# A four-layer network over eight batches: another order of its stages, the long kernel's products over four groups of TensorE, and the copy of the scores as a stage of its own

## What is computed

```
x = x + attention(norm(x), context)        8 heads over 64 keys, softmax
x = x + experts16(norm(x))                 sigmoid gates, best 4 of 16 experts, ReLU
x = x + text_layer(norm(x), context)       see below
x = x + experts8(x)                        each of 8 experts takes the best N/8 of all N = 4096 rows
```

```
K[d, l] = 2 Re( sum_n dC[d, n] exp(dtA[d, n] * l) )      256 channels, 64 states, l < 512
y       = irfft(rfft(x) * rfft(K)) + x * D_skip
```

## Time and profile before

| what | value |
|---|---|
| median of 3 runs | 1406.09 us (1405.59 to 1408.57) |
| the profiled execution | 1405.65 us |
| its span, first to last instruction | 1403.8 us |
| mean granted TensorE clock | 0.927 |
| PE busy | 1206.8 us, 86%, 5149 instructions |
| DVE busy | 920.2 us, 66%, 3415 instructions |
| ACT busy | 474.2 us, 34% |
| POOL busy | 341.8 us, 24% |
| DMA, mean | 52 GB/s |

### The profile page before, as it was taken

The page is one execution under the profiler, slowest core; times in us unless marked ns, Lnnn a source line. Parts: engine busy times, 40 slices in busy tenths (PEclk is TensorE's granted clock), DMA queues, the critical chain, the costliest instruction groups (busy, mean ns, idle before and its releaser), DMA issues. The chain is left out here.

```text
span 1403.8 us, 17324 instructions
## 1 busy us (share of the span) xinstructions
PE 1206.8 (86%) x5149; PEld 718.5 (51%) x5149; DVE 920.2 (66%) x3415; ACT 474.2 (34%) x824; POOL 341.8 (24%) x603
## 2 busy tenths in 40 slices
PE   4776967998999899899989979999687439999997
PEld 3543544555456355454546635455264326667664
DVE  6767898778778767768877877787964481211111
ACT  3535431163143326215223441531413423323221
POOL 4323220033023112203212221320203212322332
PEclk9787978999999999899999999999888759999999
DMA  8102002100300300120030040021000135533321
GB/s 281 38 15 61 19 1 69 25 1 16 92 19 1 107 18 1 49 59 19 16 92 19 1 107 15 1 62 38 1 0 0 63 107 165 144 98 91 95 39 19
DMA packets 45351, 72.51 MB, mean 52 GB/s; under 512 B 8549, under 2 KB 27208, under 8 KB 45130
## 3 DMA queue, kind: packets, MB, share of 16 engines
q1 hardware_dynamic: 39114, 62.88, 15.2%
q0 software_dynamic: 6144, 8.52, 3.4%
HBM read 58.27 MB, written 13.07 MB: 51 GB/s over the span
## 5 line engine op out<-in xcount | busy, mean ns | idle before, releaser
L843 POOL TENSOR_SCALAR ve<-mv 128x2 f32<-128x2 f32 x74 | 16.9, 228 | 509.9 <-DVE mv L1111 509.7
L1691 PE MATMUL ps<-x,keys 128*128 128x512 f32 x256 | 124.9, 613 | 4.7 <-DVE hT L1205 4.7
L1862 PE MATMUL ps<-hT,values 128*128 128x512 f32 x256 | 119.1, 594 | 0.0
L2318 PE MATMUL experts_ps<-experts_yT,experts_fc 128*128 128x512 f32 x256 | 111.9, 595 | 1.2 <-ACT experts_yT L2243 1.2
L2330 PE MATMUL experts_ps<-experts_fc,experts_hT 128*128 128x256 f32 x512 | 112.0, 379 | 0.8 <-ACT experts_hT L2255 0.8
L1691 PE MATMUL ps<-zT_second,w 128*128 128x512 f32 x224 | 104.7, 607 | 6.0 <-ACT big L1632 3.9
L2330 PEld LDWEIGHTS experts_ps<-experts_fc,experts_hT 128*128 128x128 f32 x512 | 96.6, 190 | 14.6 <-ACT experts_hT L2255 1.6
L2227 DVE SCALAR_TENSOR_TENSOR experts_o<-experts_ps,experts_wh,experts_b2w 128x256 f32<-128x256 f32 x32 | 15.5, 484 | 128.7 <-PE experts_ps L2330 128.7
L1691 PE MATMUL ps<-w,big 128*128 128x256 f32 x448 | 99.0, 379 | 0.8 <-ACT big L1632 0.8
L2255 ACT ACTIVATE experts_hT<-experts_ps,experts_b 128x512 f32<-128x512 f32 x64 | 44.0, 687 | 155.3 <-PE experts_ps L2318 155.3
L1691 PEld LDWEIGHTS ps<-w,big 128*128 128x128 f32 x448 | 84.1, 190 | 12.5 <-ACT big L1632 1.6
(11 more groups left out here) (445 smaller groups left out, 2388.9 us busy)
## 6 DMA issues: line engine op xcount, KB each, us to landing
gT<-expert_gates SPq DMA_DIRECT2D x32, 512.0 KB, 7.5
experts_fc<-in_fc1T SPq DMA_DIRECT2D x8, 1024.0 KB, 5.1
experts_fc<-in_fc2T SPq DMA_DIRECT2D x8, 1024.0 KB, 8.7
xT<-in_xT SPq DMA_DIRECT2D x8, 512.0 KB, 3.6
x<-in_x SPq DMA_DIRECT2D x8, 512.0 KB, 3.6
expert_table<-tb SPq DMA_DIRECT2D x7, 528.0 KB, 9.7
out_x<-x SPq DMA_DIRECT2D x7, 512.0 KB, 9.1
w<-in_W SPq DMA_DIRECT2D x2, 1024.0 KB, 9.1
```

Source lines behind the costliest of these rows:

```text
L843: nc.gpsimd.tensor_scalar(o, i, c, None, ALU.add).then_inc(*tick(*event))
L1691: last = nc.tensor.matmul(o, l, r_, start=start, stop=stop)
L1862: last = nc.tensor.matmul(bank("O2", k), S["values"][:, c, k * P:(k + 1) * P], hT[:, c % RING, :], start=(c == 0), stop=(c == HC - 1))
L2318: last = nc.tensor.matmul(g_bank(m), fc1[e % 3][:, k, m * P:(m + 1) * P], yT[e % 2][:, k, :], start=(k == 0), stop=(k == DC - 1))
```

## The change

It does three things.

1. The written list has another order. It has 972 entries in place of 948; the new ones are `scores_out` of each batch and `scales` 0 and 1 of each batch. No other stage is added or dropped.
2. `powers` on PE: the 32 products of a pass go to the four groups of 32 output partitions in turn, eight to each. The host puts the channels in an order that makes the result lie as before.
3. The copy of the turned scores leaves `table`. PE's turn and ACT's copy are now the stage `scores_out`; `table` keeps ACT's eight activations. POOL's nine instructions for the scales leave `scores` and become `scales`.

The code:

```diff
+QUARTERS = 4
...
             def scores(b, h):
+                w = room(b)
+                rstd_of(b, LN_EXPERTS, h, w)
+
+            def scales(b, h):
                 ts = pair(h)
                 w = room(b)
                 tr, tmr, tnm, tv, ts2, tnm2 = w.scale
-                rstd_of(b, LN_EXPERTS, h, w)
...
                     nc.scalar.activation(x3[:, t, :], x3[:, t, :], ACT.Identity, bias=w.tnm[:, t, :], scale=w.tr[:, t, :]).then_inc(*tick("x4", t))
+
+            def scores_out(b):
+                w = room(b)
                 a.wait_ge(*w.uses.at(b, "filled", "ST"))
...
             def powers(_, p):
-                lanes = slice((p // 2) * LI, (p // 2 + 1) * LI)
+                each = PC // QUARTERS
                 pe.wait_ge(*at(0, "k_pow", p))
-                for d in range(PC):
-                    last = nc.tensor.matmul(pk[lanes, p % 2, d * LJ:(d + 1) * LJ], Us[p % 2][:, d, :], WAs[p % 2][:, d, :], start=True, stop=True)
+                for r_ in range(each):
+                    place = (p * each + r_) % PC * LJ
+                    for q in range(QUARTERS):
+                        d = q * each + r_
+                        last = nc.tensor.matmul(pk[q * LI:(q + 1) * LI, p // QUARTERS, place:place + LJ], Us[p % 2][:, d, :], WAs[p % 2][:, d, :],
+                                                start=True, stop=True)
                 last.then_inc(*tick("k_taps", p))
...
-            def table(b):
+            def scores_out(b):
                 w = room(b)
                 pe.wait_ge(*at(b, "sc1"))
...
+    for name in ("log_dt", "A_reT", "A_imT", "C_reT", "C_imT"):
+        a = arrays[name]
+        arrays[name] = a.reshape(-1, QUARTERS, PASSES, PC // QUARTERS).transpose(0, 2, 1, 3).reshape(a.shape)
```

More of the change, by code:

```diff
@@ L127 @@
[L127 to L148, removed]
@@ new lines @@
+    (MID, 1, "picked", 1), (LAST, 0, "scales", 1), (LAST, 1, "film_in", 0), (LAST, 1, "film_in", 1), (MID, 2, "relu", 0),
+    (LAST, 1, "fold"), (ATTEND, 2, "spread"), (LAST, 1, "film", 0), (LAST, 1, "film", 1), (MID, 2, "mlp", 1), (MID, 2, "relu", 1),
+    (LAST, 0, "table"), (LAST, 1, "turn"), (MID, 2, "relu", 2), (LAST, 1, "transform"), (MID, 2, "text", 0), (MID, 2, "mlp", 2),
+    (LAST, 1, "product", 0), (MID, 2, "mlp", 3), (MID, 2, "mlp", 4), (MID, 2, "relu", 3), (LAST, 1, "product", 1),
@@ new lines @@
+    (ATTEND, 4, "gates", 0), (LAST, 2, "scores", 1), (ATTEND, 4, "gates", 1), (ATTEND, 4, "gates", 2), (LAST, 2, "route_experts"),
+    (LAST, 2, "turn_scores"), (ATTEND, 4, "gates", 3), (MID, 3, "text", 2), (MID, 3, "picked", 1), (LAST, 2, "shift_scores"),
+    (ATTEND, 4, "spread"), (LAST, 3, "film_in", 0), (LAST, 3, "film_in", 1), (MID, 4, "mlp", 0), (LAST, 3, "film", 0),
+    (MID, 4, "relu", 0), (MID, 4, "relu", 1), (LAST, 2, "scores_out"), (LAST, 3, "fold"), (LAST, 3, "turn"), (LAST, 3, "film", 1),
@@ new lines @@
+    (LAST, 4, "film_in", 1), (LAST, 4, "film", 0), (MID, 5, "mlp", 1), (MID, 5, "relu", 0), (LAST, 3, "table"), (LAST, 4, "film", 1),
+    (MID, 5, "relu", 1), (LAST, 3, "scales", 0), (LAST, 3, "scores_out"), (MID, 5, "relu", 2), (LAST, 4, "fold"), (MID, 5, "relu", 3),
+    (LAST, 4, "transform"), (MID, 5, "text", 0), (MID, 5, "mlp", 2), (LAST, 4, "turn"), (LAST, 4, "product", 0), (LAST, 4, "hold"),
+    (MID, 5, "mlp", 3), (MID, 5, "mlp", 4), (MID, 5, "relu", 4), (MID, 5, "mlp", 5), (MID, 5, "mlp", 6), (LAST, 4, "product", 1),
@@ new lines @@
+    (LAST, 5, "film_in", 0), (LAST, 4, "shift_scores"), (ATTEND, 6, "spread"), (LAST, 4, "table"), (MID, 6, "mlp", 1),
+    (LAST, 5, "film", 1), (LAST, 5, "film_in", 1), (LAST, 4, "scales", 1), (MID, 6, "relu", 0), (LAST, 4, "scores_out"),
+    (MID, 6, "relu", 1), (LAST, 5, "transform"), (MID, 6, "mlp", 2), (MID, 6, "relu", 2), (LAST, 5, "fold"), (LAST, 5, "turn"),
+    (MID, 6, "mlp", 3), (LAST, 5, "product", 0), (MID, 6, "mlp", 4), (MID, 6, "relu", 3), (LAST, 5, "product", 1), (MID, 6, "mlp", 5),
```

326 lines of the change are left out of this document (165 added, 161 removed).

## The result

| | us |
|---|---|
| before, median of 4 | 1405.84 (1405.31 to 1408.57) |
| changed, median of 4 | 1395.88 (1393.27 to 1397.99) |
| ratio | 0.9931, 95% interval 0.9918 to 0.9944 |
| the changed kernel's profiled execution | 1397.99, span 1396.2 |

The forecast was 1394.0. The sum came out near, but the terms did not. The passes, which were to give 7.1 of the 12.1 us, gave nothing by themselves in the old list. What lies behind batch 0's transform was priced at 3.9 us (parts 3 and 4) and gave 10.3, measured with TensorE kept busy in the lead-in (the experiments say how).

What follows compares the result with a forecast made beforehand. PE was taken as the bound from 241 to 890 us, DVE from 161 to 241. Terms -7.1, -1.1, -3.0 and -0.9 sum to -12.1 us: 1394.0 us, range 1384 to 1403.

Steps and rivals of the forecast that it cites:

- Part 3: Boundaries between batches: moved fillers cover PE's waits before the transform, the table is stored later; net -3.0 us.
- Part 4: The end: earlier score copy -2.4, `choose` in front of `ffn_add` +0.3, two GELU stages +1.2; sum -0.9 us.
- 43.7 us is all that any order can win there: From 241 to 890 us PE is busy 605.3 of 649 us and is the bound; the rest is idle.
- Part 1: `powers` products over four groups: passes fall from 3.60 to 1.1 and 2.20 to 0.7 us; 7.1 us saved.
- Rival B: Weight loads of the four groups don't overlap, so passes keep their time; -5.0 us, 1401.1; chance 0.10.
- Pass 0: First pass in the lead-in: key products behind it wait for a copy queued on ACT; 0 saved.
- Pass 3: DVE's longest wait, 3.1 us, is for this pass and PE's `mlp` stages stand behind; 2.5 us saved.
- those of PE's full stretch: Passes 4 and 5, where PE is full and DVE's two other waits are for them; 1.5 us saved each.
- Part 2: Lead-in order: `fold_film` moves ahead of pass 5, so POOL no longer slows DVE's instruction at 30.67; net -1.1 us.
- rival C: Table stores come late, DVE's `product` and then PE stand in six boundaries; +11.9 us, 1418; chance 0.08.
- Rival A: The boundary order gives nothing and DVE takes up half the passes' gain; -5.6 us, 1400.5; chance 0.18.
- Rival D: The new order fills PE's holes in the boundaries and the lead-in; -23.1 us, 1383; chance 0.16.

Runs made afterwards that it cites:

- the run without groups: The changed kernel with its passes back in one group of 32 partitions, new list kept; 0.9959 of the kernel before, 1399.13 us.
- pass 0 three times: The changed kernel with PE doing the products of pass 0 three times, same result written again; 0.9911 of the kernel before, median 1393.45 us.
- The experiment with the fillers: The kernel before with only fillers moved: `mlp` stages behind `film` 1 in boundaries 1 and 3, two GELU stages behind batch 7's films; ratio 1.0013.

## Why the prediction was right or wrong

**Bounds.** "43.7 us is all that any order can win there" was the first error. It counts only PE's idle time. PE's busy time held matmuls at half clock, and the order could win these too: the transforms alone fell from 41.8 to 30.3 us, in the run without groups as well (26.7 + 3.6). Part of it came back elsewhere: the `mlp` products rose from 124.9 to 128.3 us. (One sum is off: with part 3 at -8 the spread's lower end is 1389, not 1388.)

**Part 1.** The duration was right to a tenth (1.1 and 0.7; 1.06 and 0.74). Rival B is refuted. So is the rule of the Trainium skill, page "TensorE: Matmul & The Clock Gate", section "Part 3: Packing small matmuls", as the prediction applied it: all these products use the same rows, single weight loads still have 157 ns in the median as before, and 64 of them now fit into 1.06 us beside the products. The step that failed is "pass by pass, what reaches the chain". Pass 0 was set at 0; it cost 4 us, by the clock. Pass 3 and those of PE's full stretch were set at 2.5, 1.5 and 1.5 because DVE waited for them; that wait was the time in which POOL made its exponents (119.27 to 122.18 us at pass 3). 9.3 us of waiting went, 6.0 came back as longer DVE work and 3.4 as waiting for ACT. In place of -7.1 the groups gave +2.2 by the ratio (2.9 by the medians) in the old list and -1.4 in the new.

**Part 2.** -1.1 expected, for DVE's instruction at 30.67. POOL's exponents of pass 1 moved into the same place, so nothing left DVE's chain: its phases 0 end at 33.70 us, before at 32.46. `fold_film` then stretched the gates. I had allowed 1.1 us for that; the three rows shown alone took 2.5 more. By the experiments, all with pass 0 three times, the lead-in's order as a whole is worth 0: within 2 us either way with the old order behind it, within 4 with the new. The forecast had -1.1, with 3 either way.

**Part 3.** -3.0 expected. With batch 7's films and the end, all behind batch 0's transform is worth 10.3 us; in the two profiles 6.9 of it lie between `ffn` of batch 1 and of batch 6 (991.56 and 998.45). The term was under by more than half. 4.0 of the 6.9 us are the transforms of boundaries 3 and 4, 6.10 and 5.40 us in the old order and 3.76 and 3.83 in the new: the sum moved only the waits and left every transform at its length. The other 2.9 I can't assign. No wait of `product` for the stores of the table appeared, so rival C did not come true.

**Part 4.** The copy: 2.4 expected, 2.44 between the profiles of the two kernels, with `table` hidden just as argued. Within the new list, where `scales` come late for a `table` that stands first, it is worth 3.8. `choose` took 1.45 us (1090.78 to 1092.22), where I had 2.7, and DVE went on behind it without a wait. The two GELU stages were priced at +1.2 for sitting in front of the transform; in fact the transform fell from 6.76 to 3.62 us, and the sign was wrong. From batch 6's `ffn` to the search the changed kernel gained 3.4, in place of 0.9.

**The rest.** Rival A had the right half of the story, that DVE takes up the passes' gain. Rival D had the size of the other, that the order gives far more than 3 us, but not its reason: PE's holes in the boundaries were not filled (43.7 and 43.0 us). That 1394.0 is near the first measurement is in good part luck. By medians, groups first: they cost 2.9 us where 7.1 were to be won, and the order with the copy then gives 10.6 where the sum had 5.0 (parts 2 to 4), two errors of 10 and 6 us that nearly cancel. Order first: it gives 6.3 where the sum had 5.0, and the groups then 1.4 in place of 7.1. Both ways end at 7.7 us in place of 12.1 (the first measurement had 10.0). What one part is worth depends on whether the other is there, which a sum of parts can't show.

What stays open: which single moves of the new list keep the clock up. The experiment with the fillers shows it for batch 7 alone, in one profile, and shows that in boundaries 1 and 3 it is not the filler behind `film` 1 by itself.

## What to carry to other kernels

Read the granted clock beside every PE stage on the chain: a stage that follows a stand can take twice its time, so a shorter stage ahead of a wait can cost more than it saves. Surplus matmuls can pay where PE would stand anyway; here they stood ahead of the work before the wait, and won 4 us by moving the low clock there. Before you count a wait of VectorE as gain, look at what GpSimd does in it. And where a kernel's executions differ by several us with the clock, judge a move by medians of many runs, not by one profile.

## What was not expected

- 64 surplus products in pass 0 make the kernel 4.3 us faster (1393.45 against 1397.75 us).
- The same stand does not always cost the same. `bias` took 6.83, 3.94 and 4.03 us behind 5.00, 4.12 and 4.18 us of standing in three profiles, 6.83 behind 3.85 and behind 2.21 us in two more, and 3.63 behind 1.60 in that of the kernel before.
- Small DVE instructions suffer most beside POOL: one on 128 x 4 elements took 1.18 us in place of 0.16.
